# A mixture-of-experts block: the copy of a tile's second weights goes from VectorE to ScalarE, and one router product moves ahead of the ranks of the sixth group on TensorE

## The reference

```python
sa, ca, ga, sb, cb, gb = ...                      # from silu(c) @ wmod
h = layernorm(x) * (1 + ca) + sa
x = x + ga * linear_recurrence(h)                 # block-diagonal gates, a scan along the tokens
h = layernorm(x) * (1 + cb) + sb
logits = silu(h @ rw1 + rb1) @ rw2 + rb2          # router, 8 experts
k_prob = softmax(top 2 of the logits)
out = sum over e of we[e] * (silu(h @ w1[e] + b1[e]) @ w2[e] + b2[e])
x = x + gb * out
```

## Time and profile before

| | us |
|---|---|
| median of 3 runs | 290.1 |
| lowest and highest run | 288.29 and 291.35 |
| the profiled execution, its own time | 288.93 |
| its span, first to last instruction | 287.2 |
| PE busy in the span | 254.2 |
| DVE busy | 188.9 |
| POOL busy | 170.0 |
| ACT busy | 166.9 |

### The profile page before, as it was taken

The page is one execution under the profiler, slowest core; times in us unless marked ns, Lnnn a source line. Parts: engine busy times, 40 slices in busy tenths (PEclk is TensorE's granted clock), DMA queues, the critical chain, the costliest instruction groups (busy, mean ns, idle before and its releaser), DMA issues.

```text
span 287.2 us, 4973 instructions
## 1 busy us (share of the span) xinstructions
PE 254.2 (89%) x1187; PEld 177.0 (62%) x1187; DVE 188.9 (66%) x751; ACT 166.9 (58%) x323; POOL 170.0 (59%) x192
## 2 busy tenths in 40 slices
PE   7886997998889997999998999999999999989910
PEld 3343443354244334787877888888888888867800
DVE  3959999999999987576443444444444446868333
ACT  4169999999885445544554555555555555444400
POOL 3994311267777757777777777545554545635650
PEclk9999999999999999999999999999999999999975
DMA  7994010121131226413423433222216822290504
GB/s 212 306 333 126 19 38 26 51 66 59 46 119 54 88 74 154 126 48 111 141 71 107 110 102 110 53 76 75 65 55 194 237 74 74 75 265 4 160 0 146
DMA packets 45365, 30.51 MB, mean 106 GB/s; under 512 B 5085, under 2 KB 41999, under 8 KB 45342
## 3 DMA queue, kind: packets, MB, share of 16 engines
q1 hardware_dynamic: 39888, 21.49, 27.5%
q0 software_dynamic: 4544, 8.47, 8.9%
q10 hardware_dynamic: 910, 0.30, 0.4%
HBM read 16.39 MB, written 12.67 MB: 101 GB/s over the span
## 4 chain that ended last, share of the span: by engine, by line
PE 43%; POOL 23%; issue 14%; DVE 12%; DMA 5%; DVEq 1%; ACT 1%; POOLq 0%; ACTq 0%; SPq 0%
POOL sorted_rows L556 21%; PE bank L1263 18%; PE bank L1245 17%; PE bank L1273 3%; PE bank L1234 2%; DVE st L722 2%; DMA expert_out<-shared,tx 2%; PE bank L1150 1%; POOL shared L520 1%; PE bank L1151 1%; PE bank L1090 1%; DVE tx L816 1%; DVE hT L821 1%; DVE shared L742 1%; DMA xs<-in_L_attn_x_dram 1%
## 5 line engine op out<-in xcount | busy, mean ns | idle before, releaser
L567 POOL DMA_INDIRECT expert_out<-shared,tx x78 | 79.3, 1016 | 54.1 <-DVE shared L1036 37.6
L665 ACT ACTIVATE hT<-bank,w_t 128x256 f32<-128x256 f32 x156 | 65.5, 471 | 29.5 <-PE bank L1245 28.6
L556 POOL DMA_INDIRECT sorted_rows<-rows,sloti x64 | 64.1, 1001 | 27.2 <-issue 18.3
L1263 PE MATMUL bank<-hT,w_t 128*128 128x256 f32 x312 | 74.1, 380 | 0.0
L1245 PE MATMUL bank<-xT,w_t 128*128 128x256 f32 x312 | 74.0, 380 | 0.0
L1245 PEld LDWEIGHTS bank<-xT,w_t 128*128 128x128 f32 x312 | 56.3, 190 | 6.6 <-DVE w_t L1019 0.5
L1263 PEld LDWEIGHTS bank<-hT,w_t 128*128 128x128 f32 x312 | 56.2, 190 | 6.3
L674 ACT ACTIVATE yT<-bank,w_t 128x256 f32<-128x256 f32 x38 | 18.0, 474 | 46.3 <-PE bank L1263 46.3
L1174 PE MATMUL bank<-h2T,rw_s 128*128 128x512 f32 x64 | 33.5, 623 | 1.0 <-ACT qv L652 0.5
L1010 DVE COPY xT<-bank 128x256 f32<-128x256 f32 x39 | 16.4, 422 | 22.4 <-PE bank L1234 22.4
L1036 DVE TENSOR_TENSOR shared<-bank,tx 128x256 f32<-128x256 f32 x38 | 16.1, 424 | 19.7 <-PE bank L1273 19.6
(11 more groups left out here) (198 smaller groups left out, 326.6 us busy)
## 6 DMA issues: line engine op xcount, KB each, us to landing
tx<-sorted_rows SPq DMA_DIRECT2D x39, 130.0 KB, 2.3
w_s<-in_L_ffn_w_dram SPq DMA_DIRECT2D x16, 256.0 KB, 6.0
xs<-in_L_attn_x_dram SPq DMA_DIRECT2D x8, 256.0 KB, 5.3
rows<-rows SPq DMA_DIRECT2D x8, 256.0 KB, 2.6
av<-expert_out SPq DMA_DIRECT2D x8, 256.0 KB, 3.7
qv<-expert_out SPq DMA_DIRECT2D x6, 256.0 KB, 5.3
expert_out<-shared,tx POOLq DMA_INDIRECT x78, 2.4
sorted_rows<-padr SPq DMA_DIRECT2D x9, 130.0 KB, 2.8
```

The source lines that it names most:

```text
L556: p.indirect_dma_start(sorted_rows[:, :], bass.IndirectOffsetOnAxis(ap=sloti[:, k, t:t + 1], axis=0), rows[:, t, k, :], None).then_inc(s_d ...
L567: p.indirect_dma_start(expert_out[:, :], bass.IndirectOffsetOnAxis(ap=xr_i[:, s % U, n, D + 1:D + 2], axis=0), yo[:, s % U, n, :], None, b ...
L665: ins = nc.scalar.activation(hsT[:, u % 2, h, :], bank[4 + q][:, (h % 2) * SL:(h % 2 + 1) * SL], ACT.Silu, bias=w1_t[:, u % 2, HID + h:HID ...
L1263: ins = t.matmul(out_bank(s)[:, 0:SL], w2_t[:, u % 2, h * D:(h + 1) * D], hsT[:, u % 2, h, :], start=(h == 0), stop=(h == HC - 1))
```

## The change

VectorE no longer copies a tile's second weights. ScalarE does, with an instruction of its own queue that reads the expert's number from `tab` and copies 513 columns. In the loop it stands behind `hid:s`; the last tile's copy stands between `yb:36` and `yb:37`. In the table for tiles 0 to 10 it stands behind `hid:0` and `hid:1`, and then behind each `yb`. The first copy on ScalarE also waits for `tab`, for the weights, and for a new semaphore `s_constd`, which VectorE raises when it has put the output biases beside the weights; tile 9 waits for the second part of `tab`. `w2:s` waits for `yb:s-2`, as it did on VectorE.

Apart from that, `router:30` stood behind `rank:5` and `tx:0` in TensorE's order, and now stands ahead of both.

```diff
@@ the order of TensorE
-                router:28 router:29 rank:5 tx:0 router:30 tx:1 sum:6 l1:0 router:31 rank:6 lev:0 tx:2 l2:0 l1:1
+                router:28 router:29 router:30 rank:5 tx:0 tx:1 sum:6 l1:0 router:31 rank:6 lev:0 tx:2 l2:0 l1:1
@@ the order of VectorE, one of its lines
-                norm2:7 place:4 table1:0 w1:0 top2:5 place:5 xT:0 xT:1 w2:0 table1b:0+top2:6 place:6 w1:1 table1c:0
+                norm2:7 place:4 table1:0 w1:0 top2:5 place:5 xT:0 xT:1 table1b:0+top2:6 place:6 w1:1 table1c:0 w1:2
@@ the order of ScalarE
-                share:5 silu:29 lgc:6 silu:30 hid:0 share:6 silu:31 hid:1 lgc:7 yb:0 hid:2 yb:1 share:7 hid:3 yb:2
-                hid:4 yb:3 hid:5 yb:4 hid:6 yb:5 hid:7 yb:6 hid:8 yb:7 hid:9 yb:8 hid:10""",
+                share:5 silu:29 lgc:6 silu:30 hid:0 w2:0 share:6 silu:31 hid:1 w2:1 lgc:7 yb:0 w2:2 hid:2 yb:1 w2:3
+                share:7 hid:3 yb:2 w2:4 hid:4 yb:3 w2:5 hid:5 yb:4 w2:6 hid:6 yb:5 w2:7 hid:7 yb:6 w2:8 hid:8 yb:7
+                w2:9 hid:9 yb:8 w2:10 hid:10""",
@@ on ScalarE
+            def weights2(s, u):
+                if static(s) and s == 0:
+                    act.wait_ge(s_tab, 1)
+                if static(s) and s == EARLY:
+                    act.wait_ge(s_tab, 2)
+                e = act.value_load(tab[0:1, 1, bass.ds(s, 1)], min_val=0, max_val=NE - 1)
+                if static(s) and s == 0:
+                    act.wait_ge(s_w2, 16 * NE)
+                    act.wait_ge(s_constd, 1)
+                if not (static(s) and s < 2):
+                    act.wait_ge(s_yT_e, s - 1)
+                nc.scalar.copy(w2_t[:, u % 2, :], w2_s[:, bass.ds(e * W2E, W2E)]).then_inc(s_w2t, 1)
@@ step() of ScalarE
                         bias_out(s - 2, (u - 2) % U)
+                        weights2(s, u)
                         bias_out(s - 1, (u - 1) % U)
...
                     hidden(s, u)
+                    weights2(s, u)
@@ constants() of VectorE
-                v.tensor_copy(w2_s[:, :].rearrange("p (e w) -> p e w", e=NE)[:, :, HC * D:W2E], b2_c)
+                v.tensor_copy(w2_s[:, :].rearrange("p (e w) -> p e w", e=NE)[:, :, HC * D:W2E], b2_c).then_inc(s_constd, 1)
@@ step() of VectorE
-                if not static(s) or s < TILES:
-                    weights2(s, u)
```

More of the change, by code:

```diff
@@ L213, in adaln_block @@
         s_xnp = sem("s_xnp")
+        s_constd = sem("s_constd")
         s_root = sem("s_root")
@@ L278, in adaln_block @@
                 norm2:4 place:2 norm2:5 scan:6 scan:7+top2:3 resid:6 place:3 resid:7+root:6 norm2:6 top2:4+root:7
-                norm2:7 place:4 table1:0 w1:0 top2:5 place:5 xT:0 xT:1 w2:0 table1b:0+top2:6 place:6 w1:1 table1c:0
-                w1:2 xT:2 xT:3 w1:3 w2:1 rowsB:0 sc:0 w2:2 top2:7 xT:4 w1:4 place:7 w2:3 sc:1 w1:5 xT:5 w2:4 table2:0
-                sc:2 w1:6 xT:6 sc:3 xT:7 w2:5 w1:7 w2:6 sc:4 w2:7 xT:8 table3:0 sc:5 w1:8 w1:9 sc:6 w2:8 xT:9 w2:9
-                w1:10 xT:10 sc:7 xT:11 w1:11 sc:8 w2:10""",
+                norm2:7 place:4 table1:0 w1:0 top2:5 place:5 xT:0 xT:1 table1b:0+top2:6 place:6 w1:1 table1c:0 w1:2
+                xT:2 xT:3 w1:3 rowsB:0 sc:0 top2:7 xT:4 w1:4 place:7 sc:1 w1:5 xT:5 table2:0 sc:2 w1:6 xT:6 sc:3 xT:7
+                w1:7 sc:4 xT:8 table3:0 sc:5 w1:8 w1:9 sc:6 xT:9 w1:10 xT:10 sc:7 xT:11 w1:11 sc:8""",
             "scalar": """
@@ L678, in _ @@
                            "clamp": one_minus, "mult": multiplier, "copy": router_copy, "silu": router_silu, "lgc": logit_copy,
-                           "share": second_share, "hid": lambda s: hidden(s, s % U),
+                           "share": second_share, "hid": lambda s: hidden(s, s % U), "w2": lambda s: weights2(s, s % U),
                            "yb": lambda s: bias_out(s, s % U)})
@@ L1019, in weights1 @@
                 v.tensor_copy(w1_t[:, u % 2, :], w1_s[:, bass.ds(e * WE, WE)]).then_inc(s_w1t, 1)
[L1021 to L1028, removed]
             def scale_y(s, u):
@@ L1045, in _ @@
                            "xT": lambda s: take_x(s, s % U), "w1": lambda s: weights1(s, s % U),
-                           "w2": lambda s: weights2(s, s % U), "sc": lambda s: scale_y(s, s % U)}
+                           "sc": lambda s: scale_y(s, s % U)}
             for together in VECTOR:
```

## The result

The changed kernel takes 286.33 us (median of 6 runs, 285.81 to 288.11), the kernel before 289.59 us beside it. The ratio is 0.9895 with a 95% interval of 0.9858 to 0.9931: faster by about 1%, which is the edge that the prediction spoke of. One of the runs of before took 378.29 us and is left out of the ratio. The profiled execution of the changed kernel took 286.54 us with a span of 284.6.

The account below looks back on a forecast made before the run. TensorE, 89% busy, was taken to set most of the pace, with the chain over GpSimd up to 151.62 us. Tail -2.9 and GpSimd -0.1, other terms 0, took the median 290.1 to 287.1 us; range 285.4 to 290.0.

Parts of the forecast that it names:

- The tail: Six steps with a combine: TensorE's stalls ahead of the output transposes go, -2.9 us, bounds -1.5 and -2.9.
- The reserve of `xT`: Combine steps: without the second weights' copy, VectorE's xT ends some 0.5 us before TensorE wants its bank.
- The long stalls: Two of the six combine steps: stalls of 1.26 and 0.64 us, put down to VectorE's reading, taken as gone.
- The loop: Steps of tiles 11 to 38: ScalarE's added copy of 0.63 us fits its idle gap, step stays 3.90 us, cost 0.
- The cover of 1.72 us: ScalarE's idle time per loop step; past it every 0.1 us costs 2.8 us in 28 steps.
- GpSimd's sends: The 32 sends up to 144.82 us, with half the weights' copies gone from VectorE: -0.1 us, ends -0.6 and +0.2.
- The router product: Front part: a product of half a microsecond moves into TensorE's 1.77 us wait for the sixth group's mask; 0 us.
- Nobody waits: Front part: the silu of the moved router product comes earlier, but nothing was said to wait for it; 0 us.
- Tiles 0 to 10: Eleven copies move to ScalarE; TensorE's balance, at worst 1.1 us later, lies inside 1.21 us of idle time; 0 us.
- At 151.0 to 151.7, waiting for its rows: Start of tile 10: sign that TensorE still waits for the rows at that time, idle 0.6 to 1.7 us before.
- GpSimd gains in full: Rival: with the port free the sends lose none of the 0.6 us, tile 10 comes earlier; 286.6 us, chance 0.12.
- ScalarE as the bound: Rival: a long exposed reading makes ScalarE's loop step 4.13 us instead of 3.90; 293.9 us, chance 0.06.

Follow-up runs that it names:

- router_only: The kernel before with only router:30 moved ahead of rank:5 and tx:0, all copies left on VectorE; ratio 1.0066 on the chip with stops.
- dve_tail: The changed kernel with TensorE's old order and VectorE copying the second weights of tiles 31 to 38, ScalarE those of tiles 0 to 30; ratio 0.997.
- w2_only: The changed kernel with the router product back in its old place, behind tx:0; ratio 0.9884 on the chip with stops.
- act_tail: The changed kernel with TensorE's old order and ScalarE copying second weights only for tiles 31 to 38, VectorE for the others; ratio 0.9895.
- act_from_10: The changed kernel with TensorE's old order and VectorE copying second weights for tiles 0 to 9, ScalarE from tile 10 on; 286.77 us, ratio 0.9932.
- router_only_again: The kernel before with only the router product moved, run again on a chip like the result's; 290.24 us, ratio 0.9998.
- changed_again: The changed kernel as it is, run again beside three others on one chip; 286.03 us, ratio 0.9911 to the kernel before.
- w2_only_again: The changed kernel with the router product in its old place, run again on a chip like the result's; 285.84 us, ratio 0.985.
- copy_thrice: The changed kernel with two extra copies per step on ScalarE from tile 11 on, into a buffer nobody reads; 287.04 us, ratio 0.9905.
- changed_and_filled: The changed kernel with one more product, which nobody reads, in the place that the router product left; 285.77 us, ratio 0.9896.
- copy_twice: The changed kernel with one extra copy per step on ScalarE from tile 11 on, into a buffer nobody reads; 286.2 us, ratio 0.9878.
- w2_only_third: The changed kernel with the router product in its old place, run a third time, beside three others on one chip; 286.11 us, ratio 0.9906.

## Why the prediction was right, and where it was not

The forecast was 287.1 us; it came out at 286.3, inside the range, with the mechanism that it named. Part of the distance is not the change's: with the further runs the median of the kernel before is 289.59 and not 290.1. Against that the gain is 3.3 us, where 3.0 was forecast. Point by point:

- **The tail, -2.9 with bounds -1.5 and -2.9.** The six steps gained 26.32 - 23.37 = 2.95 us, and all behind the start of tile 10 3.0 to 3.1. `router_only` and `dve_tail` have the stalls, `w2_only` and `act_tail` have not. The reserve of `xT` was said to be 0.5 us; in the shown step it is 247.53 - 246.87 = 0.66. The long stalls as a consequence of a reading on VectorE are borne out in part: they vary between executions (1.34, 0.92 and none at the place of before's 1.08), and went with the copy. In four executions the stall rises and falls with VectorE's idle time ahead of the copy (the stall is 0.20 to 0.26 us shorter); that the reading and not something else made them long was read from the traces, not tried by itself.
- **The loop, 0.** The copy took 0.62 (0.63 was said), the reading 281 ns and hidden, the step stayed 3.90. The cover of 1.72 us was right as idle time; a copy uses 0.5 of it, not 0.63.
- **GpSimd's sends, -0.1 with ends -0.6 and +0.2.** The 32 sends and their gaps took 40.57 us in the first execution and 40.57 to 40.79 in six later ones with the copies of these tiles on ScalarE, against 41.07. So 0.3 to 0.5 us, nearer to the better end than the -0.1 that I took. But `act_from_10`, with these copies on VectorE, has 40.78 as well, and `router_only_again` 41.04. That they are what slows the sends is not shown. The Trainium skill would have given them the better end ("SBUF — State Buffer", "SBUF: two separate sides": a VectorE instruction in a two-port mode and one of GpSimd exclude each other at a shared port pair); these runs neither need that nor refute it.
- **The router product, 0.** Right for the time: 0.9998 (0.9967 to 1.003) alone on the second chip. The 1.0066 on the disturbed chip speaks for a small loss and was not found again; behind the start of tile 10 there is none to see (135.78 against 135.58). The product was taken for half a microsecond; it is two instructions in the trace and takes 1.02 (109.72 in the kernel before), so that it fills over half of the wait of 1.77, and it still fits. "Nobody waits" was not quite so: tile 0's second layer starts 11.70 us behind the first send in `changed_again` and 12.03 in `w2_only_again`. That 0.33 us is reserve for TensorE, which its wait for tile 10 swallows.
- **Tiles 0 to 10, 0 us.** This is the step that was mis-sized. It said that TensorE's balance is at worst a loss of 1.1 us inside the wait of 1.21, and that VectorE's shorter stalls help by something. The second layer of tile 0 does come later, by 12.03 - 11.55 = 0.48 us against the first send in `w2_only_again`, where TensorE waits 0.39 us for the copy on ScalarE. But behind it TensorE gains 1.1 to 1.2 us up to tile 9 in the two executions that kept the clock, `w2_only_again` and `changed_again`. With a full clock the wait for tile 10's rows grew to 2.18 us in `changed_again`, past the 0.6 to 1.7 that the prediction named, and the time is about that of before less the tail.
- **What the prediction left out:** that TensorE's clock may fall at 108 to 120 us, and that then the wait of 1.21 us is gone. "At 151.0 to 151.7, waiting for its rows" was wrong in the first profiled execution: tile 10 waited for the bank, since TensorE came late by the fall (tile 0's first layer took 2.96 us and the router product behind it 1.77, against 1.97 and 1.02 in `changed_again`). Most of what tile 10 was later than before (0.39 of 0.46 us), though, was there before the first send. The fall cost this execution at most 0.5 us. How often it happens in the runs without a profile is not known; only three of the changed kernel's 12 runs took 287 us or more.

Of the rivals, "GpSimd gains in full" (286.6) is nearer to the time than the forecast, but that is in part luck with the median of before: the gain of 3.3 us lies between the 3.0 of the forecast and its 3.5. Its mechanism holds in part. The sends are shorter by 0.3 to 0.5 us, while tile 10 starts, from the first send on, only 0.0 to 0.4 us earlier in the three executions of changed kernels that wait for its rows (47.48, 47.67 and 47.83 against 47.87). ScalarE as the bound is refuted by `copy_thrice`. No version is shown to be better than the changed kernel: 285.8 to 286.3 us for it, for `w2_only` and for the filled one lie inside each other's intervals.

## What to carry to other kernels

Ask which steps a copy makes late, not how many copies there are: eight of 39 carried this gain, because only in the combine steps was VectorE the one that TensorE waited for. A wait on a resource ahead of a stage is a reserve: what an engine gains there showed in no median here, but it can pay in the executions in which that engine comes late. Before a change of the order is blamed for a change of the clock, profile the same kernel twice.

## What the runs showed that I had not expected

- TensorE's granted clock fell to 0.50 to 0.73 at 112 to 116 us in six of nine profiled executions, the result's and eight later ones (the changed kernel, `router_only_again`, `copy_twice`, `copy_thrice`, `w2_only_third`, `act_from_10`) and stayed at 1.00 in three (`w2_only_again`, `changed_again`, `changed_and_filled`) and in the kernel before. The wait for the mask ahead of it does not decide alone: `w2_only` waited 1.78 us both times. With the router product moved it was 0.67 or 0.68 us in the four executions that fell and 0.49 in the two that did not; whether that is the cause, no run shows. The first eight products of tile 0 took 1.97 us with the full clock and 3.76 with the deepest fall.
- Copies of 513 float32 columns on ScalarE, one behind the other, cost 0.52 us each at a duration of 0.62.
- Some 40 us were lost on one chip by every kernel. The ratios of `w2_only` there and elsewhere, 0.988 against 0.985 and 0.991, still agree within their intervals.
